# The four transposes of an attention unit's sums, in two pieces among the next unit's second step

## Chip, cores and metric

One core of a Trainium2 chip. The metric is the device time of one execution in microseconds. The kernel before takes 1528.65 us, the median of 3 runs (1523.95 to 1528.92).

## What is computed

Two transformer layers over 2048 tokens of width 256 (16 heads of 16), in float32. Each layer: a layer norm with shift and scale, attention with an output projection, added under a gate; a second norm, a feed-forward part, added under a gate. In layer 0 attention is causal with a distance term and the feed-forward part is dense (704 wide); in layer 1 attention is full and the feed-forward part is a mixture of 8 experts, 2 per token, with shared experts. For attention, which is what the change touches:

```python
scores = jnp.einsum('bhqd,bhkd->bhqk', q, k) * SCALE
probs = jax.nn.softmax(scores, axis=-1)
attn = jnp.einsum('bhqk,bhkd->bhqd', probs, v)
attn = attn.transpose(0, 2, 1, 3).reshape(b, t, d)
return attn @ wo + bo
```

## The kernel before, in words

The work is a list of items in seven stages (`stages`, L439). Every engine walks the same list, takes the items that concern it, and waits for the others with semaphores. So the order of the list is the order on each engine.

Stages 1 and 3 are the attention of layer 0 and of layer 1 (`attention_walk`, L186). A **unit** n (0 to 15) is a chunk of 512 queries (n // 4) with a group of 4 heads (n % 4). A unit has **steps** k, one for each 128 keys: 4, 8, 12 or 16 in layer 0, where attention is causal, and always 16 in layer 1. A step has two **halves**, for two heads each:

- `sc`: two score matmuls of 512 columns (L1301), into three score banks in turn, and on ScalarE two exponentials (L1582). From three steps before the last unit on, scores take two banks at once, and one exponential (L1576) both.
- a part of the blocks of maxima given to this step (`max`: two matmuls at L1265, on the diagonal of layer 0 four small ones at L1271, and on VectorE one reduction at L1854). They prepare the softmax maxima of later units. `spread_blocks` (L116) spreads them over the steps by the columns that each costs; an ordinary step of layer 1 has two. L199 cuts the blocks of a step into a part before the first values, a part before the second values, and a rest.
- `pv`: the values of the step before, four heads side by side in columns of the array, one half of the queries (L1326). They add the sums and the denominators into bank 3 (`SUM_BANK`), which all units share.

Around the border between units: in step 0, behind the last values of the old unit, `oc` on ScalarE copies bank 3 to `out_sb` (L1597). The first values of the new unit, in its step 1, wait for that (L1323). `ft` is the item for what comes next: four transposes of `out_sb` on TensorE (`sums_transpose`, L1332, matmuls L1336), and on VectorE the reciprocal of the denominators (L1824) and the multiplication (L1825), in `normalise`. It stands at the end of step 1, behind the second values (L217). At the start of a chunk (n % 4 == 0) `bt`, `oq`, `op` (output projection, L1345, L1356, added at L1835) and a layer norm follow in steps 2 to 7. Some steps also have `mt` (the transpose of a unit's maxima, L1278, copied by ScalarE at L1589), put ahead of the rest of the blocks.

Blocks, `ft`, `mt`, `bt` and others take their banks from two **slots** in turn (`slot_family`, L459; the turns are dealt at L699 to L718). `open_slot` (L1139) makes TensorE wait until the slot's former user is drained; for a block that is the reduction on VectorE, for `ft` the multiplication, for `mt` the copy.

The order of one ordinary step 1 of layer 1, before: scores, block, values, scores, block, values, transposes. There are 32 units; the last one of each layer has its transposes in the list `tail` (L243), in the stage behind.

Of the kernel before, what the change touches and what calls it, by code (L numbers as in the profile page):

```python
# [16 lines left out]
P = 128  # L17
# [6 lines left out]
TPC = CH // P  # L24
# [161 lines left out]
def attention_walk(y, done):  # L186

    todo = [[b for b in pairs_of(y, n) if b not in done] for n in range(NU)]
    total = first_step(y, NU)
    first = 6 if todo[0] else 0  # L190
    out = todo[0] + [("mp", y, 0)] + todo[1][:2] + [("mt", y, 0), ("place", y, 0)] + todo[1][2:6] if todo[0] else []
    given, ready = spread_blocks(y, todo[1][first:] + [b for part in todo[2:] for b in part])
    for n in range(NU):
        steps = steps_of(y, n)
        for k in range(steps):
            s = first_step(y, n) + k
            work = given[s]

            first, second = ((len(work) + 1) // 2, len(work)) if len(work) < 3 else ((len(work) + 2) // 3, (2 * len(work) + 2) // 3)  # L199
            m, j = (n, k - 1) if k else (n - 1, steps_of(y, n - 1) - 1 if n else 0)  # L200
            if s == wide_from(y):
                out.append(("wide", y))
            out.append(("sc", y, s, n, k, 0))
            out += work[:first]
            if s:
                out.append(("pv", y, s - 1, m, j, 0))
            if n and n % NG == 0 and k in (3, 4, 5):
                out.append({3: ("oq", y, n // NG - 1), 4: ("sa", 2 * y + 1, n // NG - 1), 5: ("na", 2 * y + 1, n // NG - 1)}[k])
            out.append(("sc", y, s, n, k, 1))
            out += work[first:second]  # L210
            if s:
                out.append(("pv", y, s - 1, m, j, 1))
            if s and k == 0:
                out.append(("oc", y, n - 1))
            if k == 0 and n and n + 3 < NU:
                out.append(("rows", y, n + 3))
            if k == 1 and n:  # L217
                out.append(("ft", y, n - 1))
            if n and n % NG == 0:
                i = n // NG - 1  # L220
                if k == 2:
                    out.append(("bt", y, i))
                if k == 3:
                    out.append(("op", y, i))
                if k == 4:
                    out.append(("st", 2 * y + 1, i))
                if k == 5:
                    out.append(("nm", 2 * y + 1, i))
                if k == 6:
                    out.append(("ln", 2 * y + 1, i))  # L230
                if k == 7:
                    out.append(("lh", 2 * y + 1, i))
                if k in TOKEN_STEPS and y:
                    out.append(("tk", i, TOKEN_STEPS.index(k)))
            for m in ready.get(s, []):
                out += [("mt", y, m), ("place", y, m)]
            out += work[second:]
            out += during_attention(y, n, k)
    out += [("pv", y, total - 1, NU - 1, steps_of(y, NU - 1) - 1, z) for z in range(2)] + [("oc", y, NU - 1)]
    return out  # L240
# [207 lines left out]
            attention_walk(1, done), first, tiles, with_halves(rest)]  # L448


IN_SLOT = ("mc", "md", "mg", "mr", "ln", "qk", "v", "max", "mt", "ft", "bt", "oq", "hg", "dm", "dn", "lg", "px", "tx", "gu", "th", "dw")


SUM_BANK = 3
# [19 lines left out]
def adaln_two_layers(nc, a):  # L474
    ctx = ExitStack()
    with ctx:
# [23 lines left out]
        out_sb = sb("out_sb", [P, CH])  # L500
# [6 lines left out]
        ident = sb("ident", [P, P])  # L507
# [189 lines left out]
        for n, items in enumerate(plan):  # L697
            used = set()
            wide = False  # L699
            for item in items:  # L700
                if item[0] == "wide":
                    wide = True
                    wide_slots[item[1]] = count[0]
                own = ({"hg": "hid", "oq": "op", "dm": "dn"}.get(item[0], item[0]), *item[1:])
                if item[0] in IN_SLOT and own not in slot:
                    family = (1,) if wide else slot_family(n, item)
                    turn[family] = turn.get(family, -1) + 1
                    b = family[turn[family] % len(family)]
                    count[b] += 1
                    slot[own] = (b, count[b])  # L710
                    if b not in used:
                        first_of[own] = n
                    used.add(b)
                elif item[0] == "op":

                    family = slot_family(n, ("oq", *item[1:]))
                    turn[family] = family.index(slot[own][0])
            last_before[n + 1] = tuple(count)  # L718
# [4 lines left out]
        def filled(*item):  # L723
            return s_fill[slot[item][0]], slot[item][1]
# [4 lines left out]
        def bank_of(item):  # L729
            return SLOT_BANK[slot[item][0]]  # L730

        def bank(b):
            return psum[:, b, :]
# [404 lines left out]
        def _(pe):  # L1138
            def open_slot(item):  # L1139
                b, k = slot[item]  # L1140
                if k >= 2:
                    pe.wait_ge(s_free[b], k - 1)
                if b in (0, 2, 3) and first_of.get(item) in (2, 4):
                    y = first_of[item] // 2 - 1
                    pe.wait_ge(s_p, HG * S0[y + 1])
                    pe.wait_ge(s_oc, NU * (y + 1))
                for m, tiles in TILE_SLOTS.items():
                    if b in tiles and item in first_of:
                        pe.wait_ge(s_free[m], last_before[5][m])
                    if b == m and first_of.get(item) == 6:  # L1150
                        for k in tiles:
                            pe.wait_ge(s_free[k], count[k])
                return bank_of(item)
# [175 lines left out]
                    if z == 1:  # L1329
                        mm.then_inc(s_pv, 1)  # L1330

            def sums_transpose(item):  # L1332
                b = open_slot(item)
                pe.wait_ge(s_oc, nth["oc", item[1], item[2]])
                for t in range(TPC):
                    mm = pe.transpose(bank(b)[:, t * P:(t + 1) * P], out_sb[:, t * P:(t + 1) * P], ident[:, :])  # L1336
                mm.then_inc(filled(*item)[0], 1)

            def back_transpose(item):
                y, i = item[1:]  # L1340
# [126 lines left out]
            for it in walk:  # L1467
                if it[0] == "mc":
                    modulation_lines(it)
                elif it[0] == "md":  # L1470
                    modulation_columns(it)
                elif it[0] == "mg":
                    modulation_gates(it)
                elif it[0] == "ln":
                    ln(it)
                elif it[0] == "qk":
                    project(it)
                elif it[0] == "v":
                    value(it)
                elif it[0] == "max":  # L1480
                    if it[1:3] == (0, 0) and it[3:] == (0, 0, 0):
                        pe.wait_ge(s_const, 16 * 11)
                    max_pair(it)
                elif it[0] == "mt":
                    max_transpose(it)
                elif it[0] == "sc":
                    scores(*it[1:])
                elif it[0] == "pv":
                    values(*it[1:])
                elif it[0] == "ft":  # L1490
                    sums_transpose(it)
                elif it[0] == "bt":
                    back_transpose(it)
                elif it[0] == "oq":
                    output(("op", *it[1:]), 0)
                elif it[0] == "op":
                    output(it, 1)
                elif it[0] == "hg":
                    gate(it)
                elif it[0] == "hid":  # L1500
                    up(it)
                elif it[0] == "dn":
                    down_product(it, (1,) if ("dm", *it[1:]) in nth else (0, 1))
                elif it[0] == "dm":
                    down_product(("dn", *it[1:]), (0,))
                elif it[0] == "lg":
                    logits(it)
                elif it[0] == "mr":
                    modulation_rows(it)
                elif it[0] == "px":  # L1510
                    prefixes(it)
                elif it[0] == "tx":
                    tile_transpose(it)
                elif it[0] == "gu":
                    tile_gate_up(it)
                elif it[0] == "th":
                    tile_hidden_transpose(it)
                elif it[0] == "dw":
                    tile_down(it)
# [602 lines left out]
```

## Time and profile before

| | |
|---|---|
| median of 3 runs | 1528.65 us (1523.95 to 1528.92) |
| the profiled execution's own time | 1520.89 us |
| its span, first to last instruction | 1519.1 us |
| mean granted TensorE clock | 0.970 of full |
| attention of layer 0 / of layer 1, about | 84 to 531 us / 723 to 1352 us |

Busy time is the time in which an engine executes something, as a sum over a stretch. A row of the order of time merges instructions of one kind that follow each other: start, length from first start to last end, engine, line, operation, what is written and read, the count, and in brackets the idle time of the engine ahead of it with what ended it. PE is TensorE's matmuls, PEld its weight loads, DVE VectorE, ACT ScalarE, POOL GpSimd. Matmuls overlap: the length of one (0.39 us for 512 columns) is not what it adds, which is seen from one start to the next.

### The profile page before, as it was taken

What the parts mean: (1) busy time and instruction counts of PE and PEld (TensorE: products, weight loads), DVE (VectorE), ACT (ScalarE), POOL (GpSimd) and SP (SyncE); (2) the same over time, 40 slices, a digit from 0 to 9 for tenths busy, and PEclk for the clock granted to TensorE, in tenths of its full rate; (3) what the DMA queues carried; (4) which work ended last, traced back from release to release, by engine and by line L of the source; (5) the groups of instructions that cost most, each with busy time, mean ns of one, the idle gap of its engine ahead of it and who ended that gap; (6) DMA issues with size and microseconds to landing.
All of it is one profiled execution on the core that took longest, in us unless ns stands there. A gap on an engine that the chain in (4) does not pass through costs nothing. (4 is left out here: it accounts for less than half of the span.)

```text
span 1519.1 us, 35666 instructions
## 1 busy us (share of the span) xinstructions
PE 1390.8 (92%) x13548; PEld 584.6 (38%) x13548; DVE 1186.1 (78%) x1530; ACT 1033.9 (68%) x1976; POOL 344.4 (23%) x472
## 2 busy tenths in 40 slices
PE   6888898999899899996999999999999999989998
PEld 3543333333333255441233333333333333236665
DVE  6686797888796044899999979997999789717766
ACT  3254676777688833221899989998999889964443
POOL 2501130300100033124140028301400040055225
PEclk9997899999999999997899999999999999999999
DMA  7821120111000003223200200000000000012454
GB/s 227 162 35 40 47 72 25 38 33 50 1 2 2 1 15 71 49 39 65 91 7 7 54 7 7 7 7 6 7 7 7 7 2 2 5 67 88 143 156 145
DMA packets 56868, 68.53 MB, mean 45 GB/s; under 512 B 9819, under 2 KB 52379, under 8 KB 55963
## 3 DMA queue, kind: packets, MB, share of 16 engines
q1 hardware_dynamic: 53635, 57.87, 14.7%
q0 software_dynamic: 3072, 8.39, 1.8%
q8 instruction: 116, 1.90, 0.5%
q14 instruction: 45, 0.37, 0.1%
HBM read 45.26 MB, written 26.74 MB: 47 GB/s over the span
## 5 line engine op out<-in xcount | busy, mean ns | idle before, releaser
L1854 DVE TENSOR_REDUCE mpart<-psum 128x2 f32<-128x1024 f32 (+2 forms) x832 | 913.0, 1157 | 91.8 <-PE psum L1265 74.0
L1582 ACT ACTIVATE probs<-psum 128x512 f32<-128x512 f32 (+1 forms) x1512 | 771.9, 573 | 157.2 <-PE psum L1301 84.2
L1326 PE MATMUL psum<-probs,v_region 128*17 128x256 f32 (+1 forms) x6400 | 502.9, 387 | 18.6 <-ACT probs L1576 9.3
L1265 PE MATMUL psum<-key_region,row_region 50*128 50x512 f16 (+3 forms) x1664 | 323.3, 381 | 46.8 <-DVE mpart L1854 36.7
L1301 PE MATMUL psum<-row_region,key_region 52*128 52x512 f16 (+3 forms) x1664 | 341.5, 380 | 17.6 <-ACT probs L1582 11.9
L1301 PEld LDWEIGHTS psum<-row_region,key_region 52*128 52x128 f16 x1664 | 93.9, 93 | 335.8 <-ACT probs L1582 264.4
L1326 PEld LDWEIGHTS psum<-probs,v_region 128*17 128x17 f32 x6400 | 107.1, 95 | 220.8 <-issue 114.3
L1060 POOL TENSOR_SCALAR mp<-mx 128x16 f16<-128x16 f32 x32 | 10.3, 322 | 647.7 <-DVE mx L1865 617.3
L1265 PEld LDWEIGHTS psum<-key_region,row_region 50*128 50x128 f16 x1664 | 94.8, 94 | 149.2 <-DVE mpart L1854 85.6
L1576 ACT ACTIVATE probs<-psum 128x1024 f32<-128x1024 f32 (+3 forms) x76 | 69.7, 955 | 11.0 <-PE psum L1301 8.5
L1617 ACT ACTIVATE probs<-psum,gate_s 128x512 f32<-128x512 f32 (+1 forms) x24 | 16.4, 682 | 64.9 <-PE psum L1369 64.9
L1876 DVE SCALAR_TENSOR_TENSOR probs<-psum,up_s,probs 128x512 f32<-128x512 f32 (+1 forms) x24 | 17.9, 746 | 51.4 <-PE psum L1378 41.7
L1369 PE MATMUL psum<-hT,ffn_w 128*128 128x512 f16 (+2 forms) x216 | 52.7, 380 | 3.0 <-issue 1.8
L967 POOL TENSOR_SCALAR vare<-mv 128x4 f32<-128x4 f32 x16 | 3.7, 229 | 226.1 <-DVE mv L1768 226.0
L1088 POOL TENSOR_TENSOR hT<-attn_region,hT 128x512 f16<-128x512 f32 x30 | 34.5, 1170 | 89.0 <-ACT hT L1552 89.0
L1378 PE MATMUL psum<-hT,ffn_w 128*128 128x512 f16 (+2 forms) x216 | 52.6, 380 | 0.0
L1443 PE MATMUL psum<-ffn_w,key_region 128*128 x276 | 49.8, 314 | 1.8 <-DVE key_region L1972 1.5
L1633 ACT ACTIVATE key_region<-psum 128x176 f32<-128x176 f32 x46 | 14.6, 317 | 48.2 <-PE psum L1443 48.2
L1095 POOL TENSOR_TENSOR key_region<-probs,key_region 128x512 f16<-128x512 f32 (+1 forms) x24 | 28.1, 1171 | 70.7 <-ACT key_region L1626 70.6
L1589 ACT ACTIVATE mrow_t<-psum 128x512 f16<-128x512 f32 x32 | 19.2, 599 | 32.6 <-PE psum L1278 32.2
L1081 POOL DMA_INDIRECT key_region<-sorted_y,idx x32 | 32.0, 999 | 39.1 <-PE psum L1443 29.5
L1536 ACT ACTIVATE attn_region<-psum,modc 128x512 f32<-128x512 f32 x30 | 21.7, 774 | 26.3 <-PE psum L1197 26.3
(196 smaller groups left out, 1358.8 us busy)
## 6 DMA issues: line engine op xcount, KB each, us to landing
parts<-key_region SPq DMA_DIRECT2D x32, 256.0 KB, 3.0
key_region<-parts SPq DMA_DIRECT2D x48, 128.0 KB, 4.3
sorted_x<-in_zero SPq DMA_DIRECT2D x46, 128.0 KB, 2.6
key_region<-sorted_x SPq DMA_DIRECT2D x46, 128.0 KB
sorted_y<-key_region SPq DMA_DIRECT2D x46, 128.0 KB
row_region<-parts SPq DMA_DIRECT2D x144, 32.0 KB
key_region<-in_wmod SPq DMA_DIRECT2D x2, 1536.0 KB, 11.6
x_sb<-in_x SPq DMA_DIRECT2D x4, 512.0 KB, 8.3
```

Source lines behind the costliest of these rows:

```text
L1081: nc.gpsimd.indirect_dma_start(back[k % GB], None, sorted_y[b], bass.IndirectOffsetOnAxis(ap=idx[:, c * NT + t:c * NT + t + 1], axis=0)).t ...
L1088: ins = nc.gpsimd.tensor_tensor(hT16[tc][:, 1, c, :], mod_t[xh_buf(q, tc)][:, c, :], hT16[tc][:, 0, c, :], ALU.subtract)
L1095: nc.gpsimd.tensor_tensor(hid[y][tc % 2][0:f, c, 1, :], utmp[k % 2][0:f, :], hid[y][tc % 2][0:f, c, 0, :], ALU.subtract).then_inc(s_lo, 1)
L1265: mm = pe.matmul(bank(b + par)[:, 0:w], rows[at, g, hp, r * P:(r + 1) * P], keys[at, g * HP + hp, q * CH:q * CH + w], start=True, stop=not ...
L1301: mm = pe.matmul(bank(score_bank(y, s, e + par))[:, off:CH], keys[at, g * HP + hp, jt * P:(jt + 1) * P], rows[at, g, hp, off:CH], start=Tr ...
L1326: mm = pe.matmul(psum[32 * h:32 * h + VW, SUM_BANK, lo:hi], v_sb[:, jt, g * HG + h, :], probs[:, (S0[y] + s) % 2, h, lo:hi], start=(jt == ...
L1369: mm = pe.matmul(psum[0:f, b, :], up_gate[y][0][:, u, d, FB[y] + c * P:FB[y] + c * P + f], hT16[tc][:, v, d, :], start=(m + d == 0), stop= ...
L1378: mm = pe.matmul(psum[0:f, b + 1, :], up_gate[y][1][:, u, d, FB[y] + c * P:FB[y] + c * P + f], hT16[tc][:, v, d, :], start=(m + d == 0), s ...
L1443: mm = pe.matmul(bank(b)[:, 0:2 * FE], xT[j % 2][:, u, k, :], expert_up_gate[:, :, v, k, bass.ds(which[j] * FE, FE)], start=(m + k == 0), ...
L1576: nc.scalar.activation(probs[:, (S0[y] + s) % 2, 2 * hp:2 * hp + 2, off:CH], psum[:, b:b + 2, off:CH], ACT.Exp, scale=SCALES[y]).then_inc( ...
L1582: nc.scalar.activation(probs[:, (S0[y] + s) % 2, 2 * hp + par, off:CH], psum[:, e % 3, off:CH], ACT.Exp, scale=SCALES[y]).then_inc(s_p, 1)
L1854: V.tensor_reduce(mpart[:, n % NG, at:at + 2, q:q + 1], psum[:, b:b + 2, 0:w], AX.X, ALU.max).then_inc(drained(*item)[0], 1)
```

## The change

The item `ft` is cut in two. A new item `fa`, for TensorE alone, opens the slot, waits for the copy and makes the transposes of the first two tiles; it stands in step 1 behind the first values, ahead of the second scores. `ft` makes the other two and stands behind the second scores, ahead of the blocks of that half. VectorE's reciprocal and multiplication go with `ft`. The last unit of a layer, whose `ft` stands in `tail`, keeps all four together. The order of an ordinary step 1 of layer 1 becomes: scores, block, values, two transposes, scores, two transposes, block, values.

```diff
             if s:
                 out.append(("pv", y, s - 1, m, j, 0))
+            if k == 1 and n:
+                out.append(("fa", y, n - 1))
             if n and n % NG == 0 and k in (3, 4, 5):
...
             out.append(("sc", y, s, n, k, 1))
+            if k == 1 and n:
+                out.append(("ft", y, n - 1))
             out += work[first:second]
...
-            if k == 1 and n:
-                out.append(("ft", y, n - 1))
...
-                own = ({"hg": "hid", "oq": "op", "dm": "dn"}.get(item[0], item[0]), *item[1:])
+                own = ({"hg": "hid", "oq": "op", "fa": "ft", "dm": "dn"}.get(item[0], item[0]), *item[1:])
...
-                elif item[0] == "op":
+                elif item[0] == "op" or (item[0] == "ft" and n in (1, 3)):
 
                     family = slot_family(n, ("oq", *item[1:]))
                     turn[family] = family.index(slot[own][0])
...
-            def sums_transpose(item):
-                b = open_slot(item)
-                pe.wait_ge(s_oc, nth["oc", item[1], item[2]])
-                for t in range(TPC):
-                    mm = pe.transpose(bank(b)[:, t * P:(t + 1) * P], out_sb[:, t * P:(t + 1) * P], ident[:, :])
-                mm.then_inc(filled(*item)[0], 1)
+            def sums_transpose(item, tiles):
+                if 0 in tiles:
+                    open_slot(item)
+                    pe.wait_ge(s_oc, nth["oc", item[1], item[2]])
+                for t in tiles:
+                    mm = pe.transpose(bank(bank_of(item))[:, t * P:(t + 1) * P], out_sb[:, t * P:(t + 1) * P], ident[:, :])
+                if TPC - 1 in tiles:
+                    mm.then_inc(filled(*item)[0], 1)
...
+                elif it[0] == "fa":
+                    sums_transpose(("ft", *it[1:]), range(TPC // 2))
                 elif it[0] == "ft":
-                    sums_transpose(it)
+                    sums_transpose(it, range(TPC // 2 if ("fa", *it[1:]) in nth else 0, TPC))
```

`fa` is also added to the tuple `IN_SLOT` (L451). It takes the slot under the name of its `ft`, so the slot's turn is dealt at `fa`.

## Rows read from the trace of the kernel before

**Rows 1.** The page's first part: busy time, share of the span, instructions

```profile
PE 1390.8 (92%) x13548; PEld 584.6 (38%) x13548; DVE 1186.1 (78%) x1530; ACT 1033.9 (68%) x1976; POOL 344.4 (23%) x472
```

**Rows 2.** Busy time by unit; columns as in the first line

```profile
core 0: us, PE busy (x) PEld busy (x) DVE busy (x) ACT busy (x) POOL busy (x), PEclk, DMA share, GB/s
...
962.34:1000.23 37.89, 36.89 (x397) 12.12 (x393) 37.24 (x36) 35.00 (x67) 9.69 (x18) 1.00 0.03 7
1000.23:1038.14 37.91, 36.91 (x397) 12.10 (x393) 37.26 (x36) 35.02 (x67) 0.84 (x3) 1.00 0.03 7
...
312.91:343.41 30.50, 27.97 (x343) 9.96 (x339) 27.44 (x29) 24.08 (x51) 0.83 (x3) 1.00 0.12 31
```

**Rows 3.** Order of time, the steady part of a layer 1 unit (VectorE, TensorE, ScalarE)

```profile
1009.36 29.57 DVE L1854 TENSOR_REDUCE mpart<-psum 128x2 f32<-128x1024 f32 x26 [0.49 <-PE psum L1265]
...
1009.80 0.39 PE L1301 MATMUL psum<-row_region,key_region 52*128 52x512 f16 x2
1010.03 0.38 PE L1265 MATMUL psum<-key_region,row_region 50*128 50x512 f16 x2
1010.34 0.63 PE L1326 MATMUL psum<-probs,v_region 128*17 128x256 f32 x8
1010.90 0.39 PE L1301 MATMUL psum<-row_region,key_region 52*128 52x512 f16 x2
...
1010.23 3.28 ACT L1582 ACTIVATE probs<-psum 128x512 f32<-128x512 f32 x6 [0.42 <-PE psum L1301]
```

**Rows 4.** Order of time around the transposes of one unit in layer 1

```profile
997.83 0.60 ACT L1597 ACTIVATE out_sb<-psum 128x512 f32<-128x512 f32 x1
...
998.58 0.63 PE L1326 MATMUL psum<-probs,v_region 128*17 128x256 f32 x8 [0.40 <-ACT out_sb L1597]
...
999.13 0.39 PE L1301 MATMUL psum<-row_region,key_region 52*128 52x512 f16 x2
...
999.36 0.38 PE L1265 MATMUL psum<-key_region,row_region 50*128 50x512 f16 x2
...
999.67 0.63 PE L1326 MATMUL psum<-probs,v_region 128*17 128x256 f32 x8
...
1000.23 0.66 PE L1336 MATMUL psum<-ident,out_sb 128*128 128x128 f32 x4
...
1000.82 0.39 PE L1301 MATMUL psum<-row_region,key_region 52*128 52x512 f16 x2
1000.92 0.26 DVE L1824 RECIPROCAL rden<-psum 128x16 f32<-128x16 f32 x1
...
1001.30 1.09 ACT L1582 ACTIVATE probs<-psum 128x512 f32<-128x512 f32 x2 [0.66 <-PE psum L1301]
...
1001.67 1.23 DVE L1854 TENSOR_REDUCE mpart<-psum 128x2 f32<-128x1024 f32 x1
...
997.50 2.35 DVE L1854 TENSOR_REDUCE mpart<-psum 128x2 f32<-128x1024 f32 x2
...
999.78 1.23 DVE L1854 TENSOR_REDUCE mpart<-psum 128x2 f32<-128x1024 f32 x1
```

**Rows 5.** Order of time in layer 0, where VectorE waits for the transposes

```profile
197.80 0.66 PE L1336 MATMUL psum<-ident,out_sb 128*128 128x128 f32 x4
...
198.50 0.26 DVE L1824 RECIPROCAL rden<-psum 128x16 f32<-128x16 f32 x1 [0.42 <-PE psum L1336]
```

**Rows 6.** Order of time on VectorE at a chunk's end in layer 1

```profile
1047.86 1.23 DVE L1835 TENSOR_TENSOR x_sb<-psum,x_sb 128x1024 f32<-128x1024 f32 x1 [7.05 <-PE psum L1356]
```

**Rows 7.** Order of time, TensorE, where the maxima's transpose follows directly

```profile
842.24 0.40 PE L1278 MATMUL psum<-identh,mp 128*128 128x128 f16 x4 [0.46 <-DVE mpart L1854]
```

**Rows 8.** Order of time in a unit of layer 0

```profile
342.96 1.23 DVE L1854 TENSOR_REDUCE mpart<-psum 128x2 f32<-128x1024 f32 x1 [0.41 <-PE psum L1265]
...
344.25 0.39 PE L1265 MATMUL psum<-key_region,row_region 50*128 50x512 f16 x2 [0.18 <-DVE mpart L1854]
```

More of the change, by code:

```diff
@@ L448, in stages @@
             attention_walk(1, done), first, tiles, with_halves(rest)]
-IN_SLOT = ("mc", "md", "mg", "mr", "ln", "qk", "v", "max", "mt", "ft", "bt", "oq", "hg", "dm", "dn", "lg", "px", "tx", "gu", "th", "dw")
+IN_SLOT = ("mc", "md", "mg", "mr", "ln", "qk", "v", "max", "mt", "fa", "ft", "bt", "oq", "hg", "dm", "dn", "lg", "px", "tx", "gu", "th", "dw")
 SUM_BANK = 3
```

## The prediction, made before the changed kernel ran

> **What bounds the kernel now.** I read the page first, then busy time by unit, then the order of instructions around the transposes. The page has TensorE busy for 92% of the span, VectorE for 78%, ScalarE for 68% [rows 1]. Those are means over unlike stages, and the change touches only the two attention stages. So I cut these at the starts of the transposes (line 1336), which come once per unit. In layer 1 an ordinary unit takes 37.9 us: VectorE is busy for 37.2 of it, TensorE for 36.9, ScalarE for 35.0 [rows 2]. All three are nearly full, and VectorE is the fullest. The steady part of a unit shows the rates. VectorE's row of 26 reductions takes 29.57 us, 1.14 us each; TensorE needs 1.10 us from one pair of scores to the next (1009.80 to 1010.90: scores 0.23, a block of maxima 0.31, values 0.56), ScalarE about 1.09 for two exponentials (six in 3.28) [rows 3]. One half step holds one reduction, so VectorE sets the pace by 0.04 us and TensorE is held back through the two slots for blocks. In layer 1, then, a nanosecond matters where VectorE stands idle. It does so for only 0.65 us in such a unit (37.91 less 37.26), 0.49 of it behind the transpose of the maxima.
>
> Layer 0 is looser: a unit of 30.5 us has VectorE busy for 27.4 and TensorE for 28.0 [rows 2]. Which of them is last there alternates within a unit.
>
> **The transposes as they stand** [rows 4]. ScalarE copies the sums at 997.83. The first values of the new unit wait for that and start at 998.58. From there TensorE has no gap: scores 999.13, block 999.36, values 999.67, transposes 1000.23, scores of the next step 1000.82. So the transposes take 0.59 us of TensorE, and behind them ScalarE idles for 0.66 us. VectorE does not idle: the reduction from 999.78 covers them, and the reciprocal follows at 1000.92.
>
> **The change, part by part.**
>
> *Time on TensorE.* The number of instructions stays. Four transposes take 0.66 us with 0.27 for the last, so the starts lie 0.13 apart, and 0.20 passes from the last start to the scores. Two pieces take 2 x (0.13 + 0.20) = 0.66 us instead of 0.59: 0.07 us more per unit, 30 units (the last of each layer stays whole), 2 us at most and nothing where VectorE sets the pace.
>
> *ScalarE's idle time.* The pieces can only be free if TensorE has idle time to put them into. Behind the first values it has none. The first piece would start at 999.14, the scores of the second half at 999.47 instead of 999.13, so ScalarE idles 0.33 longer before them. The second piece starts at 999.70 (after scores, as a block does, 0.23) to 999.78 (0.31, as values follow a block). The block moves behind it to 1000.03 to 1000.11, the values to 1000.34 to 1000.42, the next step's scores to 1000.90 to 1000.98, against 1000.82. One stall of 0.66 becomes two with the same sum. I take 0 for ScalarE, +0.08 to +0.16 for TensorE locally.
>
> *VectorE's order.* This is the part with a price. The item for the second piece also stands for reciprocal and multiplication, and they move ahead of the second block of the step. Today VectorE goes from the first block's reduction (start 998.64: the row of two begins at 997.50 and its last takes 1.22) to the second's at 999.78 with no idle time. After the change it wants the transposes at 999.78. A four-piece set gives the reciprocal 0.70 us after its start, with VectorE already waiting [rows 5]; less the two transposes done earlier, 0.26, that is 0.44 after the start of the second piece, so 1000.14 to 1000.22. VectorE idles for 0.36 to 0.44 us where it had none. Reciprocal and multiplication take 0.75, to 1000.9 at least; by then the second block is long in its bank, and from there on the order of work is what it was, only late. I take 0.39.
>
> *What of it reaches the end.* In layer 1 this pattern (transposes right behind the values, 0.66 of ScalarE idle) stands twelve times, the first at 765.7, the last at 1284.0. Two of them (1038.1 and 1197.4) lead into a chunk's end, where VectorE later idles for 7.05 us [rows 6] and absorbs the shift; TensorE's +0.08 stays. Ten are left: 10 x 0.39 = 3.9 us. Two more units (841.1, 878.9) have the maxima's transpose right behind: it waits 0.46 us for the slot of the second block [rows 7] and would now get that of the transposes, some 0.2 earlier, but the next block then waits for the reduction that moved back. I take 0. The two chunk ends give 0.2, the last unit, where VectorE is not full, 0.1. Layer 1: +4.2.
>
> *Layer 0, 15 units.* In one that I followed (343.4) VectorE waits 0.41 before the second block, and TensorE 0.18 behind the transposes for its slot [rows 8]. With the new order TensorE gets the slot from the multiplication and gains those 0.18, while VectorE, idle until the transposes are there, ends 0.35 later. In another (312.9) VectorE is a whole block behind and loses nothing, but the second block finds its slot taken: TensorE +0.28. Bounds -0.2 and +0.35 each, -3 to +5 us; most of VectorE's loss falls where it has idle time later in the unit, so I take +0.1 each: +1.5.
>
> *The slot.* The first piece opens the slot before the scores, and a late slot would now delay them. At 999.14 the slot's last reduction ended at about 998.7 (1.22 from 997.50): 0.4 to spare in layer 1. No DMA is moved, SP and POOL see nothing new, and the copy of the next sums is a unit away. The tails are untouched.
>
> **Sum.** 4.2 + 1.5 = 5.7, say +5.5 us. The profiled execution took 1520.9 us (span 1519.1), so 1526.4; it lies 7.8 us below the median of the runs, 1528.65, and on the median's footing the forecast is 1534, 0.36% slower. A measurement of this kernel can tell about 0.3%, 4.6 us, so the result lies on the edge.
>
> Behind the last of the four transposes 0.20 us pass, where 0.13 lie between two of them: leaving their mode costs 0.07 by the rows. A rule of the Trainium skill, "TensorEngine Tiling (Array Packing)", Key Properties, bears on this: changing the tiling mode, not just the tile, drains the engine. From the first values to the next step's scores there are four such changes now and six afterwards, and "TensorE: Matmul & The Clock Gate" (Single matmul latency) puts a drain near 175 ns; an estimate from that is 0.35 us per unit for the two, up to 8 us in all over the sum above. The rows show the smaller price, and I go by them.
>
> **The rivals.**
>
> *The wait is absorbed (0.26).* VectorE's 0.39 falls away because it catches up before a slot is next waited for. TensorE runs at 1.10 and VectorE at 1.14 per half step, so it has little to catch up with, but the 0.49 of idle time behind the maxima's transpose could shrink. Then 0 to +3 us: 1530.
>
> *The stall really goes (0.16), faster.* ScalarE's lead of up to three score banks covers a piece of 0.33 where it does not cover 0.59. If ScalarE rather than VectorE were the true bound, each unit would get back between half of its 0.66 and all of the transposes' 0.59: 30 x 0.33 to 30 x 0.59, 10 to 18 us faster, about 1515. For it: ScalarE's six exponentials without a gap [rows 3], and the 0.66. Against it: ScalarE is idle for 2.9 us of the unit, VectorE for 0.65. It decides if VectorE's idle time at the transposes stays under 0.1 and the unit gets shorter than 37.9.
>
> *The slot is late (0.08), slower.* Where a reduction runs long before the first piece, in layer 0 above all, TensorE waits with the scores queued behind it, by half a reduction, 0.6 us: 15 units, +9, with the forecast's terms 1543.
>
> *The forecast (0.50)*: +3 to +9 us, in which I give 0.36 to more than 4.6 us.
>
> **The numbers.** Likeliest 1534. The range takes in the absorbed case and layer 0's gain (-3) at its low end, 1525, and, at its high end, the upper ends of VectorE's wait (4.4), of layer 0 (5) and of TensorE's pieces (2), 1541; the faster rival is mostly outside. Slower by over 0.3%: 0.36 + 0.08 = 0.44. Within: 0.14 + 0.26 = 0.40. Faster: 0.16.
>
> **What would show it.** Right: transposes in two pairs 0.56 apart; at each in layer 1 an idle time of VectorE of 0.3 to 0.45 before the reciprocal, released by the transposes; units of 38.2 to 38.3 us in place of 37.9; ScalarE's gap of 0.66 split into two with the same sum. Wrong: no idle time at the reciprocal, or units of 37.9 or less; or a wait of TensorE before the first piece.

## The result and the profile after

The changed kernel is slower, by little. In the runs of this set it takes 1535.24 us (median of 7, 1532.48 to 1539.25) against 1526.31 for the kernel before (7 runs, 1522.41 to 1529.26): ratio 1.0061, 95% interval 1.0041 to 1.0080, some 9 us. In a later set the ratio was 1.0056 (1.0032 to 1.0081).

The busy time by unit of the changed kernel, cut at the starts of its transposes, columns as in [rows 2]:

```profile
core 0: us, PE busy (x) PEld busy (x) DVE busy (x) ACT busy (x) POOL busy (x), PEclk, DMA share, GB/s
965.63:1004.02 38.39, 37.28 (x397) 12.07 (x393) 37.05 (x36) 34.97 (x67) 9.72 (x18) 1.00 0.03 7
1004.02:1042.39 38.37, 37.25 (x396) 12.06 (x392) 37.27 (x36) 34.95 (x67) 0.84 (x3) 1.00 0.03 6
312.86:343.61 30.75, 28.34 (x346) 10.07 (x342) 28.01 (x29) 24.11 (x51) 0.84 (x3) 1.00 0.12 34
```

An ordinary unit of layer 1 takes 38.4 us in place of 37.9. VectorE and ScalarE are busy for as long as before, TensorE for 0.34 to 0.39 us more.

The order of time around the transposes of one unit (the sums' copy, then TensorE, VectorE, ScalarE), to be laid beside [rows 4]:

```profile
1002.71 0.60 ACT L1603 ACTIVATE out_sb<-psum 128x512 f32<-128x512 f32 x1
...
1003.46 0.63 PE L1328 MATMUL psum<-probs,v_region 128*17 128x256 f32 x8 [0.40 <-ACT out_sb L1603]
1004.02 0.44 PE L1339 MATMUL psum<-ident,out_sb 128*128 128x128 f32 x2
1004.39 0.39 PE L1303 MATMUL psum<-row_region,key_region 52*128 52x512 f16 x2
1004.71 0.44 PE L1339 MATMUL psum<-ident,out_sb 128*128 128x128 f32 x2
1005.08 0.39 PE L1267 MATMUL psum<-key_region,row_region 50*128 50x512 f16 x2
1005.40 0.63 PE L1328 MATMUL psum<-probs,v_region 128*17 128x256 f32 x8
1005.96 0.39 PE L1303 MATMUL psum<-row_region,key_region 52*128 52x512 f16 x2
...
1002.38 2.34 DVE L1860 TENSOR_REDUCE mpart<-psum 128x2 f32<-128x1024 f32 x2
1005.18 0.26 DVE L1830 RECIPROCAL rden<-psum 128x16 f32<-128x16 f32 x1 [0.45 <-PE psum L1339]
...
1005.93 1.23 DVE L1860 TENSOR_REDUCE mpart<-psum 128x2 f32<-128x1024 f32 x1
...
1004.81 1.08 ACT L1588 ACTIVATE probs<-psum 128x512 f32<-128x512 f32 x2 [0.52 <-PE psum L1303]
1006.44 1.08 ACT L1588 ACTIVATE probs<-psum 128x512 f32<-128x512 f32 x2 [0.54 <-PE psum L1303]
```

Three things stand here. First, TensorE has no gap from the first values (1003.46) on, as before; from them to the next step's scores it takes 2.50 us, where it took 2.24 (998.58 to 1000.82). Second, ScalarE's one gap of 0.66 has become 0.52 and 0.54. Third, VectorE stands idle for 0.45 us before the reciprocal, with the transposes (L1339) as releaser, where nothing was idle. The row of waits gives the total in us, the number of places and the longest. Over the whole kernel this wait grew from 20.9 us in 7 places to 33.2 in 24; one long wait in the stretch of layer 0 is most of both (16.5 and 15.6). In layer 1 alone it was 1.4 us in one place and is 8.3 in 13. Before and after:

```profile
DVE rden L1824 <- PE psum L1336: 20.9, 7, 16.5
DVE rden L1830 <- PE psum L1339: 33.2, 24, 15.6
```

To see where the time goes I cut both traces at the copies of the sums (L1597 before, L1603 after), which the change doesn't move. The rows are, in this order: layer 1 from its first copy to its last, layer 0 likewise, and all behind layer 1's last copy (columns as above).

Before:

```profile
763.32:1352.44 589.12, 563.48 (x5906) 189.03 (x5903) 512.55 (x549) 527.45 (x964) 128.20 (x189) 1.00 0.04 11
94.41:528.84 434.43, 391.50 (x4532) 148.03 (x4530) 324.14 (x373) 314.83 (x626) 47.70 (x86) 0.95 0.10 28
1352.44:1519.09 166.65, 154.90 (x1178) 108.67 (x1178) 110.17 (x262) 66.98 (x172) 71.20 (x76) 1.00 0.42 127
```

After:

```profile
765.62:1360.67 595.05, 568.28 (x5906) 186.10 (x5903) 512.51 (x549) 528.20 (x964) 128.58 (x189) 1.00 0.04 11
95.29:530.52 435.23, 391.72 (x4532) 147.03 (x4530) 324.92 (x373) 314.65 (x626) 47.84 (x86) 0.96 0.10 28
1360.67:1534.28 173.61, 155.61 (x1178) 108.31 (x1178) 110.13 (x262) 66.67 (x172) 72.96 (x76) 1.00 0.40 122
```

Layer 1 is 5.9 us longer, layer 0 by 0.8, and all behind layer 1 by 7.0, though nothing there was changed (1.5 us more lie ahead of these stretches and between them). So the two spans differ by 15.2 us, 6 more than the medians do; the last 7.0 had to be explained too.

### The profile page after: what moved, and what is told of

It is laid out like the page before. It is cut to its first block and busy times, and to the rows that moved or that the text cites. A ratio compares the mean times of both kernels' runs of the same rounds, so it can differ in the third digit from the quotient of the medians.

```text
span 1534.3 us, 35666 instructions
## 1 busy us (share of the span) xinstructions
PE 1398.7 (91%) x13548; PEld 580.2 (38%) x13548; DVE 1186.9 (77%) x1530; ACT 1034.2 (67%) x1976; POOL 346.8 (23%) x472
## 5 line engine op out<-in xcount | busy, mean ns | idle before, releaser
L1466 PE MATMUL psum<-key_region 88*128 x276 | 37.8, 272 | 3.6 <-ACT key_region L1654 2.2
```

Of the source, the lines that this page charges most:

```text
L1466: mm = pe.matmul(bank(b)[:, 0:D], half_x[j % 2][0:HF, c, u, :], expert_down[0:HF, bass.ds(which[j], 1), c, v, :], start=(c + m == 0), stop ...
```

## The experiments

I had three theories. Theory 1 was the prediction's: the loss is VectorE's idle time before the reciprocal, since VectorE sets the pace. Theory 2: TensorE's longer way (2.50 against 2.24) sets the unit. Theory 3: the second half's scores come late and ScalarE pays. Diffs of the first four runs are against the changed kernel. Where one unit's time is given, it is that from the copy at 997.83 of before to the next (37.90), and the same unit in the other runs. "The six units" are the six ordinary ones of layer 1 between the copies at 922.04 and 1035.73 and between those at 1080.82 and 1194.98. Two executions of the changed kernel agree in each of the six within 0.05 us.

**whole_first**: all four transposes behind the first values, VectorE's order as in the change.

```diff
-                    sums_transpose(("ft", *it[1:]), range(TPC // 2))
+                    sums_transpose(("ft", *it[1:]), range(TPC))
                 elif it[0] == "ft":
-                    sums_transpose(it, range(TPC // 2 if ("fa", *it[1:]) in nth else 0, TPC))
+                    sums_transpose(it, range(TPC if ("fa", *it[1:]) in nth else 0, TPC))
```

> All four transposes behind the first values, none behind the scores; reciprocal and multiplication as early as in the change. Theory 1 (what costs is VectorE standing idle before the reciprocal, 0.5 us in the changed kernel): the transposes start 0.56 us after the first values and are there 0.70 us later, at +1.26, where VectorE is free at about +1.19, so its idle time shrinks to under 0.1 us and an ordinary unit of layer 1 takes 37.9 to 38.0 us (before 37.9, changed 38.4); the whole within 2 us of before. Theory 2 (TensorE's 0.26 us more between the first values and the next step's scores sets the unit): the same, since whole transposes cost 0.59 as before. Theory 3 (the scores of the second half come late, by 0.37 in the change, and ScalarE pays): here they come 0.59 late, so the unit takes 38.4 us or more and the whole is 8 us or more slower than before.

Measured: ratio to before 1.0005 (0.9982 to 1.0027), unit 37.9 us. The order of time:

```profile
997.92 0.63 PE L1328 MATMUL psum<-probs,v_region 128*17 128x256 f32 x8 [0.40 <-ACT out_sb L1603]
998.48 0.66 PE L1339 MATMUL psum<-ident,out_sb 128*128 128x128 f32 x4
999.06 0.39 PE L1303 MATMUL psum<-row_region,key_region 52*128 52x512 f16 x2
...
1000.16 0.39 PE L1303 MATMUL psum<-row_region,key_region 52*128 52x512 f16 x2
...
999.17 0.26 DVE L1830 RECIPROCAL rden<-psum 128x16 f32<-128x16 f32 x1
```

The reciprocal starts 1.25 us after the first values with no idle time in its row, and TensorE is back at 2.24. The scores come 0.59 us late, more than in the change (0.38), and it costs nothing: theory 3 falls. Moving the transposes here costs nothing that these runs can tell (layer 1 from copy to copy took 590.46 us, 1.3 more than before, but the six units only 0.03 each). What costs is the cut, or the place behind the scores, or both.

**whole_second**: all four behind the second scores, ahead of the second block (the item `fa` left out).

```diff
-            if k == 1 and n:
-                out.append(("fa", y, n - 1))
...
             out.append(("sc", y, s, n, k, 1))
             if k == 1 and n:
                 out.append(("ft", y, n - 1))
```

> All four transposes behind the second scores, ahead of the second block. Theory 1: they start at +0.88 after the first values and are there at +1.58, VectorE is free at +1.19, so it idles for 0.4 us and an ordinary unit of layer 1 takes 38.3 us; the whole 5 to 8 us slower than before. Theory 2: only one more change of mode, some 0.1 us, so 38.0 us and at most 3 us in the whole. Theory 3: no score is late in the second half, 37.9 us.

Measured: ratio 1.0018 (0.9996 to 1.0041), unit 38.2 us. VectorE's wait is there without any split, while TensorE needs only 2.34 us (997.99 to 1000.33), 0.10 more than before:

```profile
997.99 0.63 PE L1326 MATMUL psum<-probs,v_region 128*17 128x256 f32 x8 [0.41 <-ACT out_sb L1601]
...
998.87 0.66 PE L1337 MATMUL psum<-ident,out_sb 128*128 128x128 f32 x4
...
1000.33 0.39 PE L1301 MATMUL psum<-row_region,key_region 52*128 52x512 f16 x2
...
999.56 0.26 DVE L1828 RECIPROCAL rden<-psum 128x16 f32<-128x16 f32 x1 [0.31 <-PE psum L1337]
```

0.3 us per unit with only 0.10 us more of TensorE favours theory 1 over theory 2. The whole's 5 to 8 us did not come: the ratio comes to some 3 us, and its interval just takes in no change at all; layer 1 took 3.7 us more (592.82).

**split_late**: the pieces around the second values, both behind the second block.

```diff
-            if k == 1 and n:
-                out.append(("fa", y, n - 1))
...
             out.append(("sc", y, s, n, k, 1))
+            out += work[first:second]
+            if k == 1 and n:
+                out.append(("fa", y, n - 1))
+            if s:
+                out.append(("pv", y, s - 1, m, j, 1))
             if k == 1 and n:
                 out.append(("ft", y, n - 1))
-            out += work[first:second]
-            if s:
-                out.append(("pv", y, s - 1, m, j, 1))
```

> Two transposes ahead of the second values, two behind them, both behind the second block; reciprocal where it was before. TensorE pays for the split (about 0.15 us more before the next scores), VectorE gets its block on time. Theory 1: the second piece is there at about +2.49 after the first values, VectorE is free at +2.34, so it idles for 0.15 us: unit 38.05 us, the whole 1 to 3 us slower than before. Theory 2: TensorE's 0.15 us likewise, 38.05. Theory 3: scores on time, 37.9. It tells the price of the split without the place.

Measured: ratio 1.0054 (1.0033 to 1.0076), unit 38.2 us.

```profile
1005.12 0.63 PE L1328 MATMUL psum<-probs,v_region 128*17 128x256 f32 x8 [0.40 <-ACT out_sb L1603]
...
1005.91 0.38 PE L1267 MATMUL psum<-key_region,row_region 50*128 50x512 f16 x2
1006.40 0.44 PE L1339 MATMUL psum<-ident,out_sb 128*128 128x128 f32 x2
1006.77 0.63 PE L1328 MATMUL psum<-probs,v_region 128*17 128x256 f32 x8
1007.33 0.44 PE L1339 MATMUL psum<-ident,out_sb 128*128 128x128 f32 x2
1007.70 0.39 PE L1303 MATMUL psum<-row_region,key_region 52*128 52x512 f16 x2
...
1007.80 0.26 DVE L1830 RECIPROCAL rden<-psum 128x16 f32<-128x16 f32 x1 [0.24 <-PE psum L1339]
```

The split itself has a price, and a larger one than expected: a piece of two takes 0.37 us, and the first comes 0.49 after the block where values come after 0.31. TensorE needs 2.58 us to the next scores. The whole is some 8 us slower, where 1 to 3 were expected. Layer 1 accounts for 3.7 of them (592.79), no more than in whole_second; layer 0 took more here, as is shown with layer1_only.

So for six units on average the place alone costs 0.34 us (whole_second), the cut alone, behind the block, 0.22 (split_late), and both together 0.49 (the change).

**dve_late**: TensorE as in the change, VectorE's reciprocal and multiplication put back behind the second block.

```diff
+            if k == 1 and n:
+                out.append(("fn", y, n - 1))
...
-                elif it[0] == "ft":
-                    normalise(it)
+                elif it[0] == "fn" or (it[0] == "ft" and ("fn", *it[1:]) not in nth):
+                    normalise(("ft", *it[1:]))
```

> TensorE's order as in the changed kernel, but VectorE takes reciprocal and multiplication behind the second block's reduction, as before. Theory 1 as it stands (TensorE's output reaches VectorE late, whichever comes first): VectorE now waits for the second block, 0.85 us, and the slot of the transposes is held longer, so the next block comes late too: idle time 1.2 us, unit about 39.1 us. If instead only VectorE's own order were at fault: unit 37.9 to 38.1 us. Theory 2: 38.4 us, as the changed kernel.

Measured: 1556.72 us in one run (before in that set 1520.82), unit 39.3 us. The two waits of VectorE that theory 1 had worked out are both there, together 1.40 us where 1.2 were expected:

```profile
1022.66 1.23 DVE L1862 TENSOR_REDUCE mpart<-psum 128x2 f32<-128x1024 f32 x1 [0.84 <-PE psum L1269]
...
1025.06 1.23 DVE L1862 TENSOR_REDUCE mpart<-psum 128x2 f32<-128x1024 f32 x1 [0.56 <-PE psum L1269]
```

and TensorE waits 1.07 us for the slot that the transposes hold. So VectorE's own order is not at fault: the change did well to move its work along. Theory 2 had 38.4 us here, and it falls. What counts is when TensorE's next result reaches VectorE.

**dve_pad** and **pe_pad** test who sets the pace, on the kernel before. The first makes the multiplication twice:

```diff
-                V.tensor_tensor(attn_n[:, :, g * GF:(g + 1) * GF].rearrange("p t (h c) -> p t h c", h=HG),
+                for z in range(2):
+                    ins = V.tensor_tensor(attn_n[:, :, g * GF:(g + 1) * GF].rearrange("p t (h c) -> p t h c", h=HG),
...
+                    if z == 0:
+                        link(ins)
```

> The kernel before with the multiplication on VectorE made twice per unit (0.42 us and a short wait more), nothing else changed. If VectorE sets the pace of layer 1's ordinary units (theory 1), a unit takes 38.3 to 38.4 us in place of 37.9. If TensorE or ScalarE does (theories 2 and 3), 37.9 us.

The second makes the two matmuls of two blocks per unit of layer 1 twice:

```diff
-                for par in range(2):
+                for par in [0, 1] * (2 if y and r == 1 and q == 3 else 1):
```

> The kernel before with the matmuls of two blocks per unit of layer 1 made twice (2 x 0.22 us of TensorE, far from the border between units), nothing else changed. If VectorE sets the pace (theory 1), a unit stays at 37.9 to 38.0 us. If TensorE does (theory 2), it takes 38.3 us: the time that the split costs TensorE in the changed kernel, 0.26 us per unit, would then count in full.

Measured: dve_pad, unit 38.4 us (38.30 to 38.59 in the six units); pe_pad, 38.3 us (38.27 to 38.40). The first is as theory 1 said: VectorE is busy for 0.5 us more, and the six units grew by 0.45 on average. The second contradicts it: 0.44 us of TensorE cost 0.38 on average. So I asked where in the unit TensorE's time counts.

**pe_pad_mid2, pe_pad_mid3, pe_pad_front3**: one block per unit made twice or three times. The condition is `y and n >= NG and (hp, r, q) == (0, 3, 1)` for the middle of the unit and `(0, 0, 1)` for the stretch between the border and the maxima's transpose; the factor is 2, 3 and 3.

> The kernel before with one block per unit of layer 1 (units 4 to 15) made twice on TensorE, 0.22 us more, in the middle of the unit, some 10 half steps behind the maxima's transpose and some 14 ahead of the border. The padding near those two places cost 0.36 of 0.44 us. Theory 1 in the form that those runs leave: TensorE regains 0.03 us per half step on VectorE (1.10 against 1.13), so what it loses in the middle is made good before the border, and the unit stays at 37.9 us. If TensorE's time counts wherever it is spent, 38.1 us.

> The same block three times, 0.44 us more on TensorE at that place. Theory 1: the slack of that place, some 0.3 us, is used up, 0.1 to 0.15 us comes out as idle time of VectorE there and the rest is regained before the border (14 half steps, 0.4 us): unit 38.0 to 38.05 us. If TensorE's time counts wherever it is spent, 38.35 us.

Measured: 38.1 and 38.35 us. In the middle 0.22 us cost 0.19 and 0.44 cost 0.39 (means of the six units), so theory 1's claim, that TensorE makes it good against VectorE, is wrong. The trace of the kernel before had it from the start (TensorE, from the maxima's transpose to the next border):

```profile
1007.79 0.40 PE L1278 MATMUL psum<-identh,mp 128*128 128x128 f16 x4 [0.19 <-DVE mpart L1854]
...
1008.92 0.39 PE L1265 MATMUL psum<-key_region,row_region 50*128 50x512 f16 x2 [0.41 <-DVE mpart L1854]
...
1035.70 0.38 PE L1265 MATMUL psum<-key_region,row_region 50*128 50x512 f16 x2
1036.48 0.63 PE L1326 MATMUL psum<-probs,v_region 128*17 128x256 f32 x8 [0.41 <-ACT out_sb L1597]
```

Between the blocks at 1008.92 and 1035.70 no row of TensorE has idle time, so it is not held back by slots there. It makes 24 blocks in 26.78 us, 1.116 each, against VectorE's 1.132 per reduction. VectorE starts on the first of these blocks 0.44 us after it and on the last 0.82 us after it (1036.52): it falls behind by some 0.02 us per half step, too little to make TensorE wait for a slot.

> The kernel before with another block per unit (units 4 to 15 of layer 1) made three times on TensorE, 0.44 us more, but between the border and the maxima's transpose. In the middle of the unit the same 0.44 us cost 0.43: theory 1's claim that TensorE regains time there has fallen. New theory: two chains alternate. From the maxima's transpose to the border TensorE runs without a gap and its time counts in full; from the border's second block to the maxima's transpose VectorE's time counts, and TensorE waits for it at the end, 0.19 and 0.41 us. Then this padding goes into those waits: unit 37.9 to 38.0 us. If TensorE's time counts everywhere, 38.35 us.

Measured: 37.9 us, nothing for the same 0.44 us. The order of time of TensorE from the padded block (x6) to the first block behind the maxima's transpose:

```profile
1004.95 0.83 PE L1265 MATMUL psum<-key_region,row_region 50*128 50x512 f16 x6
...
1008.49 0.40 PE L1278 MATMUL psum<-identh,mp 128*128 128x128 f16 x4
1008.82 0.39 PE L1301 MATMUL psum<-row_region,key_region 52*128 52x512 f16 x2
1009.49 0.39 PE L1265 MATMUL psum<-key_region,row_region 50*128 50x512 f16 x2 [0.27 <-DVE mpart L1854]
```

The padding went into the waits for VectorE, which shrank to 0.27. In the kernel before they are 0.19 and 0.41 (rows above), and in the changed kernel still 0.19 and 0.41:

```profile
1013.18 0.40 PE L1280 MATMUL psum<-identh,mp 128*128 128x128 f16 x4 [0.19 <-DVE mpart L1860]
...
1014.31 0.39 PE L1267 MATMUL psum<-key_region,row_region 50*128 50x512 f16 x2 [0.41 <-DVE mpart L1860]
```

**layer1_only** (both items with `y == 1`, layer 0 as before) and **after_again** (the changed kernel once more):

> The change in layer 1 alone. Theory 1: layer 1's 15 units together 5.5 to 6.5 us longer than before, as in the changed kernel; layer 0's units as before within what they vary by; the whole 5 to 7 us slower than before. If layer 0 carried as much as layer 1, the whole would be only some 4 us slower.

> The changed kernel as it is, beside the same runs of before. In the first profiles the stages behind the last attention unit took 7.0 us longer than before, though nothing there was changed. If that is only what executions vary by, it is 0 to 3 us here, and layer 1's units show their 5.9 us again.

Measured: layer1_only 1.0052 (1.0029 to 1.0075) and layer 1 from copy to copy 595.22 us, 6.1 more than before; after_again 1.0056 (1.0032 to 1.0081), layer 1 595.41 us, 6.3 more, and everything behind it 168.0 us. So layer 1 carries nearly all, and the same in each execution (of before there is one trace). The stages behind it vary by themselves: 166.0 us in pe_pad, 166.5 in whole_first, 172.7 in pe_pad_front3, where only the attention of layer 1 has something added. The 7.0 us of the first pair is such a difference; what it comes from I did not look into. Layer 0 takes 431.3 us in after_again and 431.4 in layer1_only, and 426.6 in pe_pad against 434.4 in before, though these two have the same layer 0: from the whole stretch its share can't be told. From its units it can. Seven of its fifteen stretches from copy to copy (the sixth, seventh, ninth to eleventh, thirteenth and fourteenth) take the same time within 0.05 us in all six traces with the layer 0 of before. They sum to 207.09 in before and 207.04 in layer1_only, and to 208.09 and 208.10 in the two executions of the changed kernel. So the change costs these seven 1.0 us; whole_second costs them 0.3 and split_late 2.6.

## Why the prediction held, and where it did not

**The sign and the mechanism.** Forecast: 0.36% slower (+5.5 us), by VectorE's idle time before the reciprocal; a loss of more than 0.3% had a chance of 0.44. Measured: 0.61% (+8.9 us), interval 0.41 to 0.80, so the forecast was too low. That the medians, 1534 and 1535.24, are only 1.2 us apart is luck in part: the forecast stood on 1528.65 for the kernel before, which in the set of the result took 1526.31. Of the 8.9 us some 6 are in layer 1 and about 1 in layer 0; the rest no unit shows, and the interval, from about 6.3 us up, does not ask for it. The idle time is in the trace, whole_second brings it back without a split, and whole_first takes it away together with the loss. The faster rival had as its condition an idle time under 0.1 us and a shorter unit; both failed, and its reason with them: the pieces never found idle time of TensorE, and in whole_first the scores for ScalarE come 0.59 us late without making the unit longer. The absorbed rival failed too, as 0.47 of the 0.52 us by which the reciprocal is late came out in the unit. Of the late slot no wait shows in layer 1: the first piece starts 0.56 us after the first values, at once. In layer 0 TensorE waits before the transposes for 1.2 us in all, in 6 places, where it was 0.5 in 3; the rival had 9.

**The terms that were mis-sized.** The pieces were put at 0.33 us each from the spacing inside a set of four. They take 0.37. The way from scores to the second piece was put at 0.23 to 0.31 and took 0.32. So TensorE's +0.08 to +0.16 was +0.26, and VectorE's delay, taken as 0.39, was 0.52: its first reduction began at 1003.52, would have let the next start 1.14 later, and the reciprocal came at 1005.18. (The row shows 0.45 idle, as a reduction lasts a little longer than the 1.14 between two of them.) Layer 1 gave 5.9 to 6.3 us where the sum had 4.2: in the first execution the ten ordinary units lost 4.8 where it had 3.9, the two with the maxima's transpose behind the transposes 0.3 each where it had 0, the two chunk ends 0.4 where it had 0.2, and the last unit 0.1. Layer 0 was put at +1.5, and its seven steady units show 1.0. ScalarE's two gaps, forecast to keep the sum of 0.66, sum to 1.06: ScalarE has the same work in a longer unit, and whole_first shows that its late scores are not the cause. TensorE's measured 0.26 us lies between my upper bound of 0.16 for this stretch and the estimate of 0.35 that I had worked out from the Trainium skill, "TensorE: Matmul & The Clock Gate", Single matmul latency. The runs do not say how much of the 0.26 is a drain and how much comes from cutting the set.

**The step that failed.** I wrote that VectorE sets the pace in layer 1 and that TensorE is held back through the two slots. The first holds for a part of the unit only, and the second not in the unit's middle. I had read 0.04 us between the two rates from a single half step of TensorE (1.10); over 24 of them it is 0.02, and it never adds up to a wait for a slot. The padding runs leave this picture. From the first block behind the maxima's transpose to the second block of the border step TensorE is the chain that counts, its only idle time there being the 0.4 us for the copy; 0.44 us more of its work cost 0.39 (pe_pad_mid3). From there to the next maxima's transpose VectorE's work counts (0.5 us more cost 0.45, dve_pad), and TensorE, which waits for it for 0.6 us at the end, took 0.44 us more for nothing (pe_pad_front3). The border is where one chain hands over to the other: in the kernel before VectorE comes free (999.78) just as the second block is there (999.36 and 0.38 long). That makes one number decide: how long after the first values VectorE gets what it must take next. The unit's growth is the mean of the six units against 37.98 before:

| | reciprocal or block, after the first values | against before | six units of layer 1 | grown by |
|---|---|---|---|---|
| before | reduction of the block starts at 1.20 | | 37.9 to 38.1 | |
| whole_first | reciprocal at 1.25 | +0.05 | 37.9 to 38.1 | 0.03 |
| whole_second | reciprocal at 1.57 | +0.37 | 38.2 to 38.5 | 0.34 |
| changed | reciprocal at 1.72 | +0.52 | 38.4 to 38.7 | 0.49 |
| split_late | reciprocal at 2.68, where 2.34 was due | +0.34 | 38.1 to 38.3 | 0.22 |

The delay agrees with the growth within 0.03 us in three rows and within 0.12 in split_late. TensorE's own extra time (0, 0.10, 0.26 and 0.34) does not: it is far below the growth in whole_second and in the change. The prediction's sum came out near because it priced this same delay. Its reason for TensorE's part costing nothing was wrong, but that part lies ahead of the handover and is already inside the delay.

## What to carry to other kernels

Before cutting an operation into pieces, price two things apart: the cut, and the new place. Here the engine had no idle time at either place, and a gap on another engine behind the operation did not mean that the cut could win it back. Take an engine's rate from many periods and not from one. Where two engines are both nearly full, find the place where one hands over to the other and ask what reaches the second engine later. And pad each engine in turn at several places of the period: a row without gaps on both engines does not say which of them counts there.

## What the runs showed of the hardware

A transpose pair is dearer than half of a set of four: 0.37 us from the first start to the next instruction, where the four take 0.58 to 0.59. From the start of a pair of scores to the transposes behind it 0.32 us passed, against 0.22 to 0.23 to a block; from the start of a block to the transposes behind it 0.49, against 0.31 to values (split_late). Executions of the unchanged stages behind the attention took 166.0 to 173.6 us, a spread of 7.6, more than the whole change cost layer 1, so a difference of two spans has to be cut by stage before it is read.
